# Many-head attention on one core: scores made twice, by query for the row maxima and by key for the probabilities

## What is computed

```python
x = x + L0_attn(layernorm(x), qk, ov)                     # stage 0: one head, causal
x = x + L0_xattn(layernorm(x), ctx, ctx, mask, ...)       # stage 1: 16 heads, masked
x = x + L0_ffn(layernorm(x), w_router, ...)               # stage 2: routed blocks
x = x + L1_attn(layernorm(x), w_qkv, b_qkv, w_o, b_o)     # stage 3: 16 heads, no mask
x = x + L1_xattn(layernorm(x), ctx, ctx, tokens, ...)     # stage 4: 16 heads, masked
x = x + L1_ffn(layernorm(x), gate_weight, ...)            # stage 5: experts
```

```python
def L1_attn(x, ...):                    # 16 heads of 16 features
    q, k, v = split(x @ w_qkv.T + b_qkv)
    attn = softmax(einsum('blhc,bmhc->bhlm', q, k) / 16)
    return einsum('bhlm,bmhc->blhc', attn, v) @ w_o.T + b_o + x

def L1_xattn(q, k, v, cell, ...):       # 16 heads of 16 features
    qh, kh = rotary(heads(ln(q) @ w_q.T + b_q)), rotary(heads(ln(k) @ w_k.T + b_k))
    mask = (i >= j) & (cell[i] == cell[j])
    a = softmax(where(mask, einsum('bhqd,bhkd->bhqk', qh, kh) / 4, min))
    return ln(einsum('bhqk,bhkd->bhqd', a, vh)) @ w_o.T + b_o
```

## Time and profile before

| | |
|---|---|
| runs | 771.14, 773.27, 773.70 us; median 773.27 |
| the profiled execution | 771.75 us; span of its trace 769.8 us |
| granted TensorE clock, mean of the span | 0.998 |
| PE busy | 739.7 us, 96%, 6077 instructions |
| PEld | 612.4 us, 80% |
| DVE | 533.8 us, 69%, 1422 |
| ACT | 440.2 us, 57%, 1275 |
| POOL | 334.5 us, 43%, 461 |

### The profile page before, as it was taken

One profiled execution on the slowest core, in us unless ns is written; L12 is line 12 of the kernel. 1 busy time (PEld: TensorE's weight loads), 2 busy tenths in 40 slices (PEclk: granted clock), 3 DMA queues, 4 the chain that ended last, 5 costly groups with the idle time before them and its releaser, 6 DMA issues.

```text
span 769.8 us, 17237 instructions
## 1 busy us (share of the span) xinstructions
PE 739.7 (96%) x6077; PEld 612.4 (80%) x6077; DVE 533.8 (69%) x1422; ACT 440.2 (57%) x1275; POOL 334.5 (43%) x461
## 2 busy tenths in 40 slices
PE   8999999999899999999999999999999999999997
PEld 7897777776787888887878787777877777889995
DVE  5666788888663554458777777778888888756545
ACT  3445677777532222237777767676667676457740
POOL 2323334434232411234332216667768855726540
PEclk9999999999999999999999999999999999999999
DMA  8903244230265555630000003000000001235538
GB/s 311 384 2 87 73 119 102 77 77 2 66 191 139 143 146 152 190 40 1 2 1 2 1 2 124 15 15 15 16 14 29 29 30 42 89 109 170 172 122 304
DMA packets 67043, 69.48 MB, mean 90 GB/s; under 512 B 22448, under 2 KB 57648, under 8 KB 65936
## 3 DMA queue, kind: packets, MB, share of 16 engines
q1 hardware_dynamic: 63552, 59.03, 26.0%
q0 software_dynamic: 3408, 9.34, 3.6%
HBM read 38.96 MB, written 29.40 MB: 89 GB/s over the span
## 4 chain that ended last, share of the span: by engine, by line
PE 71%; DVE 16%; POOL 3%; DMA 3%; issue 3%; ACT 3%; SPq 1%; ACTq 0%; POOLq 0%; DVEq 0%
PE pj L379 10%; PE pj L372 8%; PE pj L466 8%; PE ov L541 6%; PE sc L528 6%; PE sc L455 6%; PE ov L477 4%; DVE mx L1022 4%; PE sc L722 4%; PE pj L366 4%; DVE pT L1029 3%; PE sc L673 2%; PE ov L730 2%; PE sc L450 2%; PE ov L379 2%
## 5 line engine op out<-in xcount | busy, mean ns | idle before, releaser
L1549 ACT ACTIVATE pr<-sc,mx 128x128 f32<-128x128 f32 x768 | 217.4, 397 | 85.2 <-DVE mx L1022 83.2
L1022 DVE TENSOR_REDUCE mx<-sc 128x4 f32<-128x512 f32 x192 | 125.7, 682 | 27.1 <-PE sc L455 25.8
L466 PE MATMUL pj<-idn,pr 128*128 128x128 f32 x768 | 121.9, 283 | 7.5 <-ACT pr L1549 2.4
L466 PEld LDWEIGHTS pj<-idn,pr 128*128 128x128 f32 x768 | 84.3, 141 | 46.2 <-issue 26.1
L1029 DVE COPY pT<-pj 128x512 f32<-128x512 f32 x128 | 87.5, 686 | 23.2 <-PE pj L466 23.0
L1569 ACT ACTIVATE hT<-sc,vecs 128x256 f32<-128x256 f32 x64 | 30.3, 474 | 90.8 <-PE sc L528 90.8
L1746 POOL TENSOR_SCALAR ve<-mv 128x2 f32<-128x2 f32 x40 | 13.8, 344 | 155.3 <-DVE mv L951 154.9
L541 PE MATMUL ov<-W,hT 128*128 128x256 f32 x256 | 61.4, 383 | 2.1 <-DVE hT L1116 2.1
L528 PE MATMUL sc<-xnT,W 128*128 128x256 f32 x256 | 60.5, 380 | 0.0
L1532 ACT ACTIVATE pT<-pj 128x512 f32<-128x512 f32 (+1 forms) x72 | 41.8, 590 | 27.7 <-PE pj L466 27.4
L1771 POOL TENSOR_SCALAR kM<-kraw,vecs 128x256 f32<-128x256 f32 x64 | 34.8, 558 | 51.8 <-ACT kraw L1532 51.8
(11 more groups left out here) (227 smaller groups left out, 1515.1 us busy)
## 6 DMA issues: line engine op xcount, KB each, us to landing
sorted_x<-more_xT SPq DMA_DIRECT2D x15, 1152.0 KB, 7.6
kM<-sorted_x SPq DMA_DIRECT2D x39, 129.0 KB, 2.1
cT<-in_ctxT SPq DMA_DIRECT2D x16, 256.0 KB, 3.5
pr<-kept_at SPq DMA_DIRECT2D x32, 128.0 KB, 3.3
pT<-kept_at SPq DMA_DIRECT2D x32, 128.0 KB, 3.3
W<-in_w SPq DMA_DIRECT2D x2, 1024.0 KB, 13.0
cT<-in_ctx SPq DMA_DIRECT2D x8, 256.0 KB, 3.7
W<-in_w_gu SPq DMA_DIRECT2D x1, 2048.0 KB, 8.1
```

The lines of the kernel that those rows point to most:

```text
L466: last = tr(bank[b][:, i * S:(i + 1) * S], pr[n % 4][:, i, :], idn[:])
L1022: v.tensor_reduce(mx[n % 4][:], four(b), AX.X, ALU.max, negate=True).then_inc(mx_done, 1)
L1549: last = a(pr[n % 4][:, i, :], bank[b][:, i * S:(i + 1) * S], ACT.Exp, bias=mx[n % 4][:, i:i + 1])
```

## The change

In stages 3 and 4 the scores are made twice. **By query** (`by_query`, L485 of the changed kernel): as before, queries on the partitions of the result; they serve the row maxima alone. **By key** (`by_key`, L514): the operands exchange places, keys are on the partitions of the result, and the exponentials of it are what the product with values takes, without turning. A maximum by query cannot be a bias by row there. So it is subtracted inside the product: queries `qM` and keys `kM` are now both held once for even and once for odd heads, in 32-row strips of which the 16 rows of the other head are free; in `kM` one of the free rows is 1 (`unit`), and in `qM` that row takes the negated maxima. To get them there, VectorE writes the 16 columns of a half's maxima in one tile, TensorE turns it (`turn_maxima`, L494, one transpose to 16x128), ScalarE copies it out (`mxT`), and SyncE issues two DMAs (`shift`) into `qM`'s rows. By query and its maxima run half a unit ahead of by key.

With that go: `turn_probs` and `copy_probs` (stage 1 keeps them), `overtaken` for these stages, and the biases of the exponentials, which become one instruction over a whole bank. The masks of stage 4 are needed in both forms: `mb1`, and `mbT1` with keys on the partitions, made by two more VectorE instructions over 128x2048 in units 5 and 6 and a DMA (`causT`). VectorE adds the mask of some banks by key (`DVE_MASKED`) and takes mask and maximum in one pass for some banks by query (`DVE_MAXED`). Splitting queries and keys by head moves from GpSimd and VectorE to ScalarE (`apart`, `turned`, with scales that hold a zero for the other head's rows). Projections, normalisations and rotations for it move a quarter of a unit up to a whole unit earlier. Outputs are turned back (`turn_out`, now L567) behind the scores by key. The blank rows go out in another order: five pairs of DMAs at the start, six beside the contexts of stage 1, four in stage 2, and the contexts of stage 4 are loaded from the same loop as the shifts. `pT` now lies in `hT[1]`, so a wait on it in GpSimd's `scatter` is gone, and `keep` lies in `pr`, `oT` and `hd`.

```diff
@@ def program
-        qT = [sb(f"qT{r}", [P, C, T]) for r in two]
+        qM = [sb(f"qM{r}", [P, C, 2, T]) for r in two]
+        qT = [t[:, :, 0, :] for t in qM]
-        kM = [sb(f"kM{r}", [P, C, 2, 2, S]) for r in two]
+        kM = [sb(f"kM{r}", [P, C, 2, T]) for r in two]
-        mx = [sb(f"mx{r}", [P, 4]) for r in range(4)]
+        mx = [sb(f"mx{r}", [P, H]) for r in two]
+        mxT = [sb(f"mxT{r}", [H, S]) for r in two]
-        ACT_TURNS = {1: (2, 6), 3: (2, 6), 4: (1, 2, 5, 6)}
-        DVE_MASKED = {1: (2, 3, 6, 7), 3: (), 4: (3, 7), 5: ()}
+        ACT_TURNS = {1: (2, 6)}
+        DVE_MAXED = {4: (3, 7), 5: (3, 7), 6: ()}
+        DVE_MASKED = {1: (2, 3, 6, 7), 3: (), 4: (2, 3, 6, 7), 5: (3, 7), 6: ()}
-            return 5 if U >= 4 * PAIRS + 6 else stage(U)
+            return stage(U) if U < 4 * PAIRS + 2 else 5 if U < 4 * PAIRS + 4 else 6
@@ TensorE
+            def by_query(U, j):
...
+                for c in range(C):
+                    for i in two:
+                        for b, strip, added in sides:
+                            o = (2 * c + i) * S
+                            last = mm(bank[b][:, o:o + S], qM[U % 2][strip, c, i, s], kM[U % 2][strip, c, i, s],
+                                      start=not added, stop=True, skip_group_check=True)
...
+            def turn_maxima(U, j):
+                b, n = begin("pj", "mT", U, j)
+                pe.wait_ge(drained[b], n - 1)
+                pe.wait_ge(*emptied("n", U, 4 * j + 3))
+                tr(bank[b][0:H, 0:S], mx[j][:], idn[:]).then_inc(filled[b], 1)
+            def by_key(U, j):
...
+                pe.wait_ge(s_shift[j], 32 * (att(U) - PAIRS + 1))
...
+                            last = mm(bank[b][:, o:o + S], kM[U % 2][strip, c, i, s], qM[U % 2][strip, c, i, s],
+                                      start=not added, stop=True, skip_group_check=True)
@@ TensorE, half(U, j)
-                Z, k = earlier(U, j)
+                Z, N = earlier(U, j), following(U, j)
...
+                if shifted(N[0]):
+                    by_query(*N)
...
+                if shifted(U):
+                    by_key(U, j)
+                if shifted(N[0]):
+                    turn_maxima(*N)
+                if shifted(Z[0]):
+                    turn_out(*Z)
@@ VectorE
+            def maxima(U, j):
...
+                    if f == 4 and n in DVE_MAXED[masking(U)]:
+                        side = mb1[:, 2 * p + j, :]
+                        for c in range(C):
+                            for i in two:
+                                some = bank[b][:, (2 * c + i) * S:(2 * c + i + 1) * S]
+                                last = v.tensor_tensor_reduce(some, some, side, -1.0, 3.0e38, ALU.add, ALU.min, dst[:, c, i:i + 1])
+                    else:
+                        last = v.tensor_reduce(dst, bank[b][:, :].rearrange("p (c i s) -> p c i s", c=C, i=2), AX.X, ALU.max,
+                                               negate=True)
+                if U == 5:
...
+                    v.tensor_tensor(mbT1[:], tk, along(tq[:], S), ALU.not_equal).then_inc(s_eq, 1)
+                if U == 6:
...
+                    v.scalar_tensor_tensor(mbT1[:], mbT1[:], NEG, over(causT[:], B), ALU.mult, ALU.add).then_inc(s_mb, 1)
@@ ScalarE
-                for i in range(4):
-                    last = a(pr[n % 4][:, i, :], bank[b][:, i * S:(i + 1) * S], ACT.Exp, bias=mx[n % 4][:, i:i + 1])
+                a(pr[n % 4][:], four(b), ACT.Exp).then_inc(drained[b], 1)
+            def apart(dst, name, W, scale, shift):
...
+                for c in range(C):
+                    for i in two:
+                        last = a(dst[:, c, i, :], bank[b][:, c * T:(c + 1) * T], ACT.Identity, bias=shift[:, 2 * c + i:2 * c + i + 1],
+                                 scale=V(scale, i))
@@ SyncE
+            for i in range(5):
+                blank_rows(i)
             for p in range(2, PAIRS):
                 sp.wait_ge(*full("v", PAIRS + p - 2))
                 sp.dma_start(cT[p % 2][:], ctxT[:, :, p * T:(p + 1) * T]).then_inc(s_ct[p % 2], 16)
-                blank_rows(p - 2)
+                blank_rows(p + 3)
+            def shift(U, j):
+
+                sp.wait_ge(*emptied("mT", U, j))
+                for i in two:
+                    sp.dma_start(qM[U % 2][16 * (1 - i):P:32, :, i, j * S:(j + 1) * S],
+                                 mxT[j][8 * i:8 * i + 8, :]).then_inc(s_shift[j], 16)
```

More of the change, by code:

```diff
@@ L299, in overtaken, with shifted, masked @@
         def overtaken(U, j):
-            return stage(U) in (1, 3, 4) and (U % PAIRS, j) != (PAIRS - 1, 1)
+            return stage(U) == 1 and (U % PAIRS, j) != (PAIRS - 1, 1)
+        def shifted(U):
+            return stage(U) in (3, 4)
+        def masked(U, n):
+            before = sum(len(DVE_MASKED[masking(V)]) for V in range(PAIRS, U) if attends(V))
+            return before + sum(m <= n for m in DVE_MASKED[masking(U)])
         def masking(U):
-            return 5 if U >= 4 * PAIRS + 6 else stage(U)
+            return stage(U) if U < 4 * PAIRS + 2 else 5 if U < 4 * PAIRS + 4 else 6
         def att(U):
@@ L844, in part3 @@
                     turn_dropped(U + 1)
-                if whole(U + 2):
+                if stage(U + 2) in (0, 1, 2):
                     turn_x(U + 2)
@@ L852, in part3 @@
                     center(3)
-                if attends(U) and not overtaken(U, 1):
+                if U == 2 * PAIRS - 1:
                     turn_probs(U, 7)
@@ L1057, in values @@
                                     ALU.add).then_inc(drained[b], 1)
-            def queries(W, i):
-                b, n = spot["q", W]
-                dve.wait_ge(filled[b], n)
-                for o in range(C):
-                    last = v.tensor_scalar(qT[W % 2][:, o, :], bank[b][:, o * T:(o + 1) * T], (0.25, 0.0625)[i],
-                                           bq[i][:, o:o + 1], ALU.mult, ALU.add)
-                last.then_inc(drained[b], 1)
             def residual(what, U):
@@ L1419, in alone0 @@
                     keep_hidden(U, 0)
-                if stage(U + 2) in (0, 1, 2, 3) and stage(U) not in (0, 1):
+                if stage(U + 2) in (0, 1, 2) and stage(U) not in (0, 1):
                     x_norm(U + 2)
```

496 lines of the change are left out of this document (290 added, 206 removed).

## The result

The changed kernel takes 766.74 us (median of 6 runs, 764.20 to 767.67) against 771.92 before (6 runs, 769.25 to 773.70). The ratio is 0.9926, 95% interval 0.9908 to 0.9945: 0.7% faster, or 5.2 us. The forecast was 764, from a sum of -8.8 and a time before of 773.27.

A forecast was written before the change was run, and what follows sets the result against it. TensorE was taken to set the pace in stages 3 and 4. Its terms summed to -13.3 us, waits and other terms brought this to -8.8; from a 773.27 median the forecast was 764, range 757 to 770 (chance 0.50).

The forecast's parts named there:

- A block of scores by key: TensorE, stages 3 and 4: 32 instructions of 128 columns, 1.09 us each block; 32 blocks add 34.9 us.
- changes of shape: TensorE drains when its tiling mode changes: five to seven per half, three priced; all seven would add some 3 us.
- A preload's 0.25: Stage 4: TensorE preloads 108 masks in place of 52, 56 more at 0.25 us each, +13.8 us.
- The rival at 796: Loads of strips bound TensorE's scores: 64 blocks at +0.5 us, so 796 us; chance 0.05.
- the rival on ScalarE: ScalarE sets the pace in stages 3 and 4, exponentials at 0.60, queries at 0.48: +13.6, 777 us; chance 0.13.
- The shift: Two DMAs carry copied maxima into rows of the queries; hidden with 3.0 and 4.0 us to spare in stage 3, cost 0.
- The items that it had added up to 11.5 us: Last unit, without turning and copying: 11.5 us against 17.0 before, beyond TensorE's sum a gain of some 2.5.
- other small costs: Small costs missed, such as first units of a stage and queues; chance 0.09, about half of them near no change.
- +2 for the maxima in one pass: Stage 4: VectorE's mask and maximum take 1.4 us, not 0.60, a bank; some +2 in four j=1 halves.
- +1.5 in units 36 and 37: VectorE's next maxima sit behind GpSimd's two rotations, four scatters and the normalisation's inverse: +1.5 us.
- +1 for the first maxima among stage 2's block weights: Stage 3's first maxima fall among stage 2's block weights: +1 us, between 0 and 3.
- the rival of more gain: Waits of 7 us are covered and those of stage 4's later units go too: 757 to 751 us; chance 0.15.

The follow-up runs named there:

- experiment 2: Changed kernel with stage 3's queries split by head on VectorE, not ScalarE, in two instructions over 128x512: 759.97 us, ratio to the kernel before 0.9854.
- experiment 8: Changed kernel with unused products of ones in four TensorE waits (end of stage 1, unit 24, two near the end): 762.99 us.
- experiment 9: Kernel before the change with unused products of ones in three of its TensorE waits (end of stage 1, two near the end): 769.28 us.
- experiment 3: Changed kernel with unit 26's key projection ahead of unit 24's second scores by key, not behind them: 766.24 us.
- experiment 1: Changed kernel with stage 3's queries split by head on VectorE, not ScalarE, in four instructions of 128x256: 764.96 us.
- experiment 4: Changed kernel with VectorE, not TensorE, adding the masks of banks 3 and 7 by key in units 36 to 39: 762.35 us.
- experiment 5: Changed kernel with each stage 4 mask in front of scores by query preloaded twice, 56 more TensorE instructions: 775.56 us.
- experiment 7: Changed kernel with nine unused products of ones in front of the last pairs' routed products: 765.18 us.
- experiment 10: Changed kernel with the blank rows issued where they were before the change: 765.69 us.
- experiment 6: Changed kernel with SyncE issuing and awaiting a 4 KB DMA before each pair of shift DMAs: 774.33 us.

## Why the prediction was right, and where it was not

**TensorE's terms.** A block of scores by key was put at 1.09 and takes 1.11; one by query, forecast as unchanged, 1.11 against 1.07. The turned maxima were put at 0.23 and take 0.11, the lower bound. Against that stand changes of shape, of which the sum had left out all but three: the four projections of a unit take 1.92, 1.82, 1.92 and 1.76 (the last where nothing waits, experiment 2), 0.5 more than four times 1.74. TensorE's row of a stage 3 unit was forecast as 15.8; with all waits gone it is 15.99 (experiment 2). A preload's 0.25 holds, with 0.21 to 0.22 where it follows its like.

**Loads of strips.** The rival at 796 fell at the first row of PEld: a block takes 1.11 and not 1.6.

**ScalarE.** The unit was forecast at 16.0 with 0.2 of waits, and took 16.71 with 0.72. What failed here is the row taken for the queries: 0.36 each from stage 1's two instructions; here they took 0.48, the upper price that stood in the rival on ScalarE. With it came a wait that the prediction did not have: the value projection takes the bank that the queries are read from. By my estimate from these rows, at 0.36 each the queries would have been out at 399.8, when TensorE first needs that bank (399.34 and 0.44); at 0.48 they were out at 400.16. The exponentials' 0.50 was right (2.07 for four, 1.91 to the next start). So the rival's mechanism came in part: 0.7 in each of the five steady halves with j = 0 of stage 3, none in stage 4.

**The shift** is hidden in all steady units, as said. In the last unit it is not: 1.1 us. The prediction had priced that unit with terms that leave the DMA out, though next to nothing stands between its maxima and its scores by key. The items that it had added up to 11.5 us (one block by query with four masks, maxima, two by key, two sets of exponentials) stand between the masks at 623.41 and the last values' product at 638.78, 15.37 us: besides the 1.13 for the DMA and 0.90 for divided heads, TensorE has two sets of values' products, the router and a projection there.

**First units.** Unit 24 waits 0.59 and 1.72, unit 30 waits 1.14. None was priced; they had a chance of 0.09 together with other small costs. The steady half's room is 0.1 us over the ring of banks, so in unit 24 a half with one projection fewer could only wait.

**VectorE.** Mask and maximum in one pass take 1.15 for a bank (four instructions from 495.17 to 496.32), between the bounds of 0.6 and 2.4 and near the 1.4 taken:

```profile
495.17 0.29 DVE L1122 CUSTOM_DVE_ANT_0 sc<-sc,mb 128x128 f32<-128x128 f32 x1
...
496.12 0.14 DVE L1122 DVE_READ_ACCUMULATOR2_ANT mx<- 128x1 f32 x1
496.32 0.69 DVE L1168 TENSOR_TENSOR X<-pj,X 128x512 f32<-128x512 f32 x1
```

Stage 0 is 1.1 us longer (the first values' product of stage 1 at 75.56 against 74.42), as put. From one values' product to that of the next unit, units 32 to 36 take 19.5, 19.3, 21.1, 21.6 and 21.8 us, before 19.5, 19.7, 22.6, 21.4 and 21.5. The forecast of 19 and 22 was near. Of the waits that it had put in and around stage 4, +2 for the maxima in one pass and +1.5 in units 36 and 37, the rows show 1.8, and at other places: two sets of masks are held back by 0.5 us each (1.23 for three at 500.46, 1.22 at 480.97), and 0.8 stand in unit 38. Otherwise no wait of TensorE over 0.15 us is left in units 31 to 37, where the kernel before had 2.4 us of them. Of the +1 for the first maxima among stage 2's block weights nothing shows: from 333 to 351 us TensorE does not wait.

**The sum.** Without falls of the clock the change is worth some 6, of -8.8 in the sum. The profiles of experiments 8 and 9, the changed kernel and the one before without falls, split it by the starts of the values' products:

| stretch | before | changed | difference | in the sum |
|---|---|---|---|---|
| to the first of stage 1 | 74.19 | 76.09 | +1.9 | +1 |
| to the first of unit 24 | 273.68 | 275.53 | +1.9 | +1 |
| unit 24 to unit 32 | 143.02 | 138.86 | -4.2 | -12.3 |
| unit 32 to the last | 150.00 | 145.53 | -4.5 | +1.4 |
| the rest | 125.75 | 124.92 | -0.8 | 0 |
| span | 766.64 | 760.93 | -5.7 | -8.9 |

Of the first +1.9, 0.8 is there when stage 0's first products start and varies by itself. The second +1.9 is in the main the first scores by key (1.1) and the wait of 0.59. The last column splits the prediction's own terms by stage (-8.9 by rounding).

So the total was near, but not its parts. The step that failed is the one that gave stage 3 eight units of 16.0 us, 1.54 less each. Only four are steady (25 to 28), and they gain 0.83, since two waits on the queries and the turned heads cost 0.72 where 0.2 was put, and TensorE's own row is 15.99 and not 15.8. Unit 24 takes 0.4 more than before, 29 takes 0.2 more, 30 the same with its wait of 1.14, and 31 takes 1.4 less. Stage 4, where no gain was forecast but in the last unit, gains in units 34, 37 and 38 (1.5, 2.3 and 1.1). In unit 34 waits of 1.3 us of the kernel before are gone, as the rival of more gain had it; waits don't explain units 37 and 38, and their cause stays open. These two errors offset each other, and that the total came near owes something to luck. Some of stage 4's work was moved into stage 3 as well; how much of the two differences is that, I have not split, and no run moves the projections or rotations alone.

The time was helped by one thing more: the kernel before took 771.92 beside the changed one, 1.35 less than the 773.27 that the forecast started from. From that start the 5.2 would give 768.1, still inside 757 to 770. TensorE's busy share in stage 3 stayed above the 95% under which the forecast would have been wrong: 136.93 of 141.60 us from 351.6 to 493.2.

What may lie between 6 and the 5.2 of the medians is the clock: new waits come at places where it may fall. No term had it, because no row of before shows a fall in stages 3 and 4, though its own trace has one at 200 us, behind two waits of 1.0.

## What to carry to other kernels

Price every half of a hand-written pipeline that lacks a neighbour, the first and the last of a stage: steady units hide waits that those cannot, and a gain in a steady unit counts only as often as there are steady units. Where a ring of PSUM banks passes through two engines twice, add up the ring before moving TensorE's work about; in the one half tried here (experiment 3) another order below its length did not help. And on TensorE, where it sets the time, a wait can cost more than its length, so look at the granted clock behind it, and try filling what cannot be removed.

## What was not expected of the hardware

TensorE's granted clock falls to 1.2 GHz for 3.4 us in some executions behind waits of 1.0 to 2.4 us, and in others, behind the same wait, it does not (the changed kernel's six have mean clocks of 0.996 and 0.998). Unit 24 with its wait of 1.72 to 1.75 ran on at 1.00 in the profiles of experiments 1, 2, 4, 5, 7 and 10 and fell in that of the changed kernel:

```profile
354.00:357.00 3.00, 2.17 (x40) 2.03 (x41) 0.85 (x3) 1.01 (x3) 0.00 (x0) 1.00 0.00 0
357.00:360.40 3.40, 3.40 (x71) 2.67 (x69) 2.21 (x7) 3.10 (x8) 0.93 (x2) 1.00 0.04 7
```

(windows of experiment 4). The wait for `routed_y` near the end, 1.4 to 2.4 us, is followed or met by a fall in seven profiles (the changed kernel, experiments 1, 2, 4, 5, 6 and 10) and not in two (1.61 in the kernel before, 1.84 in experiment 3). So the wait is a condition, and what else decides is open. The fall in unit 24 cost 1.7 us (a half of 9.06 and not 7.38), where TensorE is busy throughout. Useless products in the waits take the mean clock to 0.999 or 1.000 in all six runs, and bring their spread from 3.5 us to 0.6.
